# A two-layer graph attention kernel: the mean of a row without edges as one more product, and part of layer 1's weights on ScalarE

## The reference, cut to what matters

```python
h = relu(layernorm(x))                       # x: 8192 x 128
Whs, Wht, Whc = h @ Ws, h @ Wt, h @ Wc
e = Whs @ Wht.T                              # 8192 x 8192
alpha = softmax(where(adj > 0, e, -9e15))    # adj: int32, 0 or 1, about 8 ones in a row
x = x + alpha @ Whc                          # layer 0
h = relu(layernorm(x))
Wh = h @ W
e = leaky_relu((Wh @ a1)[:, None] + (Wh @ a2)[None, :], 0.2)
attention = softmax(where(adj > 0, e, -9e15))
x = x + elu(attention @ Wh)                  # layer 1
```

## Time and profile before

| | us |
|---|---|
| runs | 1568.74, 1573.38, 1574.76; median 1573.38 |
| profiled execution | 1571.87, span 1570.0 |
| PE busy | 1332.9 (85%) |
| DVE busy | 1372.5 (87%) |
| ACT busy | 854.9 (54%) |
| mean granted TensorE clock | 0.948 |

### The profile page before, as it was taken

One profiled execution on the slowest core, in us unless ns is written; L12 is line 12 of the kernel. 1 busy time (PEld: TensorE's weight loads), 2 busy tenths in 40 slices (PEclk: granted clock), 3 DMA queues, 4 the chain that ended last, 5 costly groups with the idle time before them and its releaser, 6 DMA issues. The chain is left out here.

```text
span 1570.0 us, 77864 instructions
## 1 busy us (share of the span) xinstructions
PE 1332.9 (85%) x31819; PEld 1156.7 (74%) x31819; DVE 1372.5 (87%) x2732; ACT 854.9 (54%) x1552; POOL 1.5 (0%) x11
## 2 busy tenths in 40 slices
PE   1736899999999999999999988686987887898885
PEld 1525778888888888888888877456887887887885
DVE  5776799999999999999999995357999899999997
ACT  1835566666676676676766665483432333333332
POOL 0000000000000000000000000000000000000000
PEclk9977899999999999999999999898998999999998
DMA  6058889999999999999999993102233232232331
GB/s 222 0 207 312 303 299 368 366 372 373 364 366 369 372 368 368 366 371 368 369 368 370 367 372 109 52 0 89 84 99 94 71 97 83 91 99 65 104 96 37
DMA packets 114303, 363.19 MB, mean 231 GB/s; under 512 B 11504, under 2 KB 44528, under 8 KB 81392
## 3 DMA queue, kind: packets, MB, share of 16 engines
q1 hardware_dynamic: 114160, 361.02, 64.5%
HBM read 319.03 MB, written 41.94 MB: 230 GB/s over the span
## 5 line engine op out<-in xcount | busy, mean ns | idle before, releaser
L799 PE MATMUL ps<-arena 128*128 128x129 f32 x2048 | 268.2, 293 | 31.7 <-DVE arena L1462 31.5
L1454 DVE TENSOR_SCALAR arena<-arena 128x128 f32 (+1 forms) x1024 | 267.9, 338 | 27.0 <-ACT arena L1040 26.7
L799 PEld LDWEIGHTS ps<-arena 128*128 128x128 f32 x2048 | 256.3, 207 | 41.2 <-DVE arena L1462 36.0
L722 PE MATMUL ps<-arena 128*128 128x129 f32 x2048 | 252.6, 282 | 2.8 <-DVE y_t L1361 1.7
L722 PEld LDWEIGHTS ps<-arena 128*128 128x128 f32 x2048 | 240.6, 196 | 10.4 <-issue 2.3
L1287 DVE TENSOR_SCALAR arena<-arena 128x2048 fp8e4<-128x2048 int32 x192 | 234.8, 1224 | 6.2 <-PE ps L679 2.5
L976 ACT ACTIVATE arena<-ps 128x512 f32<-128x512 f32 x256 | 153.4, 599 | 132.9 <-PE ps L664 132.8
L788 PE MATMUL ps<-arena 128*32 128x131 f16 x8192 | 157.9, 230 | 38.9 <-issue 28.2
L970 ACT ACTIVATE arena<-ps 128x512 f16<-128x512 f32 x256 | 153.6, 600 | 55.9 <-PE ps L652 55.8
L702 PEld LDWEIGHTS ps<-arena 128*128 128x128 f16 x2048 | 136.7, 98 | 63.4 <-issue 3.5
L1040 ACT ACTIVATE arena<-ps 128x393 f32<-128x393 f32 (+1 forms) x384 | 150.0, 462 | 54.9 <-PE ps L788 54.9
(11 more groups left out here) (147 smaller groups left out, 1378.0 us busy)
## 6 DMA issues: line engine op xcount, KB each, us to landing
arena<-in_adjB SPq DMA_DIRECT2D x256, 1024.0 KB, 7.5
sel_pick<-arena SPq DMA_DIRECT2D x64, 256.0 KB, 9.5
sel<-arena SPq DMA_DIRECT2D x64, 256.0 KB, 9.5
arena<-sel_pick SPq DMA_DIRECT2D x64, 256.0 KB, 3.1
arena<-sel SPq DMA_DIRECT2D x64, 256.0 KB, 2.7
x_t<-in_x SPq DMA_DIRECT2D x64, 64.0 KB, 7.4
x_mid<-y_t SPq DMA_DIRECT2D x64, 64.0 KB, 7.7
arena<-x_mid SPq DMA_DIRECT2D x8, 512.0 KB, 4.4
```

Source lines behind the costliest of these rows:

```text
L722: last = nc.tensor.matmul(pv_ps, p_T[:, s * P:(s + 1) * P], v_sel[:, b, s, :], start=(s == 0), stop=(s == SB - 1), skip_group_check=True)
L799: last = nc.tensor.matmul(xv_ps[b], w_msk[:, b, s, :], x1_sel[:, b, s, 0:VW], start=(s == 0), stop=(s == SB - 1))
L1454: last = nc.vector.tensor_scalar(w_raw[:, s, :], own, x1_sel[:, b, s, D + 2:D + 3], x1_sel[:, b, s, D + 1:D + 2], ALU.mult, ALU.max)
```

## The change

Three things are changed.

1. **The mean as first product.** The value of a row without edges no longer comes from a flag. The mean, times 2^-90, is split into three bfloat16 parts in three groups of partitions (`mean_parts`), with 2^-90 itself in the denominator's column. One bfloat16 matmul of ones with these rows starts each weighted sum, in both layers. Next to real weights 2^-90 is lost in rounding; without edges it is all there is, and the division gives the mean. So `denominator` is one reciprocal read from PSUM, the base `u_t` is gone from `finish`, and in layer 1 `finish_a` has neither the flag's product nor its addition. The bound that `decide` puts on small denominators goes from exp(-50) to exp(-30).
2. **Four of sixteen raw weights on ACT** (`bend`): slot groups 6 and 7 of each half. max(a*r, b) is written as relu(a*r - b) + b: a Relu with two per-partition operands and an Identity with one. For this each gathered row has one more column, -b (`XW` 132 instead of 131), and `w_raw` has two buffers. The masked product waits for `w_act` too.
3. **The finish of a batch in four pieces**: `finish_a` behind the first tile of the next batch, `above_zero` behind the third, `below_zero` behind the fourth, `finish_b` behind the fifth. SP loads x8 and stores a batch's result in the seventh tile instead of the fourth.

```diff
@@ PE: weigh; weigh_rows likewise with mean_rows[1]
+                    nc.tensor.matmul(pv_ps, ones_b[:, :], mean_rows[0], start=True, stop=False, skip_group_check=True)
...
-                                            start=(s == 0), stop=(s == SB - 1), skip_group_check=True)
+                                            start=False, stop=(s == SB - 1), skip_group_check=True)
@@ PE: selected_keys
+                pe.wait_ge(rows_ready, 2)
@@ SP: batch_io
-                    if u == 3:
+                    if u == 6:
@@ ACT
+            def bend(t, b, h):
+
+                act.wait_ge(xg_evac, t * 6 + (3 if h == 0 else 6))
+                wait(act, w_ready, t * 2 + (h - 3))
+                act.sem_inc(act_settled, 1)
+                own = r_row[:, bass.ts(t, P)]
+                for s in BENT:
+                    k = 8 * h + s
+                    last = nc.scalar.activation(w_raw[b][:, k, :], own, ACT.Relu, bias=x1_sel[:, b, k, D + 3:XW],
+                                                scale=x1_sel[:, b, k, D + 2:D + 3])
+                last.then_inc(bend_done, 1)
+                act.wait_ge(bend_done, t * 2 + (h + 1))
+                for s in BENT:
+                    k = 8 * h + s
+                    last = nc.scalar.activation(w_raw[b][:, k, :], w_raw[b][:, k, :], ACT.Identity,
+                                                bias=x1_sel[:, b, k, D + 1:D + 2])
+                last.then_inc(w_act, 1)
...
+                    for h in range(2):
+                        bend(t, u % 2, h)
@@ DVE: denominator and finish of layer 0
-                nc.vector.tensor_scalar(no_edge[:, 0, bass.ds(t, 1)], den, 0.0, None, ALU.is_equal
-                                        ).then_inc(flag_done, 1)
-                dve.wait_ge(flag_done, t + 1)
-                nc.vector.scalar_tensor_tensor(dens[:, bass.ds(t, 1)], den, TINY, no_edge[:, 0, bass.ds(t, 1)],
-                                               ALU.max, ALU.max).then_inc(den_done, 1)
-                dve.wait_ge(den_done, t + 1)
                 settle()
-                nc.vector.reciprocal(inv[:, 3:4], dens[:, bass.ds(t, 1)]).then_inc(inv_done, 1)
+                nc.vector.reciprocal(invs[:, bass.ds(t, 1)], pv_ps[:, D:VW]).then_inc(inv_done, 1)
...
-                nc.vector.scalar_tensor_tensor(u_t[:, 0, :], mean_v[:, 0, :], no_edge[:, 0, bass.ds(t, 1)],
-                                               x_t[:, b, :], ALU.mult, ALU.add).then_inc(base_done, 1)
@@ DVE: the mean's parts, made once before each layer
+            def mean_parts(rows, left, done):
+
+                done(nc.vector.tensor_copy(rows[:, 0:D], left[:, :]))
+                done(nc.vector.tensor_tensor(left[:, :], left[:, :], rows[:, 0:D], ALU.subtract))
+                nc.vector.tensor_copy(rows[32:64, 0:D], left[32:64, :])
+                done(nc.vector.tensor_copy(rows[64:P, 0:D], left[64:P, :]))
+                done(nc.vector.tensor_tensor(left[64:P, :], left[64:P, :], rows[64:P, 0:D], ALU.subtract))
+                done(nc.vector.tensor_copy(rows[64:P, 0:D], left[64:P, :]))
+                nc.vector.memset(rows[96:P, :], 0.0)
+                nc.vector.memset(rows[32:64, D:VW], 0.0)
+                nc.vector.memset(rows[64:96, D:VW], 0.0)
+                nc.vector.memset(rows[0:32, D:VW], UNIT).then_inc(rows_ready, 1)
@@ DVE: finish_a of layer 1
-                nc.vector.tensor_tensor(fin[:, 1, :], flag, tot[:, :, D], ALU.add).then_inc(fin1_done, 1)
-                nc.vector.tensor_tensor(y8[:, :, :], flag.unsqueeze(2).to_broadcast(full),
-                                        mean_v[:, 1, :].unsqueeze(1).to_broadcast(full), ALU.mult
-                                        ).then_inc(h8_part, 1)
...
-                nc.vector.tensor_tensor(y8[:, :, :], y8[:, :, :], tot[:, :, 0:D], ALU.add).then_inc(h8_part, 1)
@@ DVE: step of layer 1
-                    if u == 1 and (not isinstance(j, int) or j):
-                        finish_b(j - 1)
+                        if u == 2:
+                            above_zero(j - 1)
+                        if u == 3:
+                            below_zero(j - 1)
+                        if u == 4:
+                            finish_b(j - 1)
```

More of the change, by code:

```diff
@@ L28 @@
 SHIFT = 50.0
-TINY = 1e-30
+UNIT = 2.0 ** -90
+NONE = 2.0 ** 84
+DEPTH = 30.0
 EPS = 1e-5
@@ L38 @@
 QB = P // SLOT
-XW = D + 3
+XW = D + 4
+BENT = (6, 7)
 NO_EDGES = struct.unpack("<f", bytes([0xB0] * 4))[0]
@@ L95, in gnn_kernel @@
         mx_b = part(TOP + 2304, P)
+        mean_rows = [part(at, 65, BF16)[:, 0:VW] for at in (END, TOP + 2560)]
+        mean_left = part(END + 65, P)
         no_edge = part(TOP + 2432, 2 * TILES).rearrange("p (k t) -> p k t", k=2)
@@ L114, in gnn_kernel @@
         W1A = VS + 2 * SB * XW
-        w_raw = part(W1A, 2048).rearrange("p (s n) -> p s n", n=P)
+        w_raw = [part(at, 2048).rearrange("p (s n) -> p s n", n=P) for at in (W1A, 5120)]
         w_msk = part(W1A + 2048, 4096).rearrange("p (r s n) -> p r s n", r=2, n=P)
-        assert W1A + 6144 <= 6 * N
+        assert W1A + 6144 <= TOP + 2304 and 5120 + 2048 <= VALS
         m_in = part(MASK + 2048, 1024, F16).rearrange("p (r n) -> p r n", r=2)
@@ L279, in gnn_kernel @@
         w_made = sem("w_made")
+        bend_done = sem("bend_done")
+        act_settled = sem("act_settled")
+        w_act = sem("w_act")
         w_ready = sem("w_ready")
@@ L797, in weigh_rows @@
                     wait(pe, tot_in, t - 1)
+                    nc.tensor.matmul(xv_ps[b], ones_b[:, :], mean_rows[1], start=True, stop=False,
+                                     skip_group_check=True)
                 for s in range(8 * h, 8 * h + 8):
                     last = nc.tensor.matmul(xv_ps[b], w_msk[:, b, s, :], x1_sel[:, b, s, 0:VW],
-                                            start=(s == 0), stop=(s == SB - 1))
+                                            start=False, stop=(s == SB - 1), skip_group_check=True)
                 last.then_inc(xv_done, 1)
             def selected_keys():
+                pe.wait_ge(rows_ready, 2)
                 def step(j, u):
@@ L1381, in tile_step @@
                 if there(i, 4):
-                    denominator(d, b)
+                    denominator(d)
                 if there(i, 0):
@@ L1451, in weights @@
                     dve.wait_ge(xg_evac, t * 6 + (3 if h == 0 else 6))
-                    wait(dve, w_ready, t * 2 + (h - 1))
-                    for s in range(8 * h, 8 * h + 8):
-                        last = nc.vector.tensor_scalar(w_raw[:, s, :], own, x1_sel[:, b, s, D + 2:D + 3],
-                                                       x1_sel[:, b, s, D + 1:D + 2], ALU.mult, ALU.max)
+                    wait(dve, w_ready, t * 2 + (h - 3))
+                    for s in range(8):
+                        if s not in BENT:
+                            k = 8 * h + s
+                            last = nc.vector.tensor_scalar(w_raw[b][:, k, :], own, x1_sel[:, b, k, D + 2:D + 3],
+                                                           x1_sel[:, b, k, D + 1:D + 2], ALU.mult, ALU.max)
                     last.then_inc(w_made, 1)
@@ L1459, in weights, with chain_rows @@
                     dve.wait_ge(w_made, t * 2 + (h + 1))
+                    dve.wait_ge(w_act, t * 2 + (h + 1))
                     wait(dve, xv_done, t * 2 + (h - 3))
                     settle()
-                    nc.vector.scalar_tensor_tensor(w_msk[:, b, at, :], m_in8[:, b, at, :], 0.0, w_raw[:, at, :],
+                    nc.vector.scalar_tensor_tensor(w_msk[:, b, at, :], m_in8[:, b, at, :], 0.0, w_raw[b][:, at, :],
                                                    ALU.is_gt, ALU.mult).then_inc(w_ready, 1)
+            made = [0]
+            def chain_rows(ins):
+                made[0] += 1
+                ins.then_inc(parts_made, 1)
+                dve.wait_ge(parts_made, made[0])
             def compare():
@@ L1500, in finish_b, with below_zero @@
                                                ).then_inc(elu_part, 1)
+            def below_zero(j):
                 dve.wait_ge(h8_exp, j + 1)
                 nc.vector.tensor_scalar(e8[:, :, :], e8[:, :, :], 1.0, -1.0, ALU.min, ALU.add).then_inc(elu_part, 1)
+            def finish_b(j):
                 dve.wait_ge(elu_part, j * 2 + 2)
@@ L1506, in selected_keys @@
             def selected_keys():
+                mean_parts(mean_rows[1], mean_v[:, 1, :], chain_rows)
                 def step(j, u):
                     weights(j * STEPS + u, u % 2)
-                    if u == 0 and (not isinstance(j, int) or j):
-                        finish_a(j - 1)
-                    if u == 1 and (not isinstance(j, int) or j):
-                        finish_b(j - 1)
+                    if not isinstance(j, int) or j:
+                        if u == 0:
+                            finish_a(j - 1)
+                        if u == 2:
[4 more added lines that the diff above has]
+                            finish_b(j - 1)
```

59 lines of the change are left out of this document (30 added, 29 removed).

## The result

| | before | after |
|---|---|---|
| median of the runs compared | 1571.89 | 1518.41 (1515.84 to 1534.86) |
| ratio, 95% interval | | 0.968 (0.961 to 0.974) |
| profiled execution | 1571.87, span 1570.0 | 1534.86, span 1533.0 |
| PE, DVE, ACT busy | 1332.9, 1372.5, 854.9 | 1311.9, 1272.6, 1043.3 |

The forecast was 1519.

What follows compares the result with a forecast made beforehand. It took DVE to bound layer 1, PE close behind, and DMA to hold layer 0. Gains of 46.5 us (layer 1), 2.3 (last finish_a) and 4 (layer 0 and seams) off 1571.87 gave 1519 us; 8-in-10 range 1499 to 1542.

Steps and rivals of the forecast that it cites:

- Layer 1's pace: Layer 1: PE becomes the pace instead of DVE, with weighted sums 6.12 us apart.
- the eight activations: Layer 1, ACT: four Relus and four Identities per tile take 3.2 us (2.8 to 3.7), which barely fits.
- halfway between two rows: Layer 1, ACT: Identities 0.29 us apart, the middle between a copy without operands (0.18) and a Relu (0.41).
- The limits of 3.3 and 3.6 us: Layer 1, ACT: room for its activations until its next sum comes late (3.3), until its work exceeds PE's step (3.6).
- rival B: Layer 1: ACT sets the pace with a tile of 6.5 us, 24 us given back, 1543 us; chance 0.12.
- Jumps: Layer 1's loop: six jumps cost PE 5.4 us each beyond a tile, 32.4 in all, no longer hidden.
- the slower sum behind: Layer 1: the first sum after each jump runs at a lower clock, 0.4 us each, 2.6 for six.
- 3.4 of the jump: Layer 1 before the change: the part of a jump that reaches DVE, in its batch sum of 61.4 us.
- behind the layer's last sum: End of layer 1: the last finish_a is shorter by 2.3 us.
- The start and the mean's parts: Ahead of layer 0's sweep: small steps that make the mean's parts add 2.6 us, 0 if loads hide it.
- the missing hundredth: Layer 0: DMA share 0.99 leaves 0 to 8 us to gain, 5 taken; layer 0 and the seams together -4.
- Rival A: Layer 0: DMA share is not capacity and PE sets the pace, 24 us more off, 1495 us; chance 0.09.

Runs made afterwards that it cites:

- e11: The changed kernel with layer 1's batches written out and six of sixteen raw weights on ACT instead of four: 1533.81 us, ratio 0.977.
- e7: The changed kernel with layer 1's loop over batches written out on all engines, so no jump is taken in it: 1486.92 us, ratio 0.949.
- e10: The kernel before with the change in layer 1 only, and layer 1's batches written out: 1491.06 us, ratio 0.948.
- e5: The kernel before with layer 0's fourth adjacency chunk loaded for the first tile only and used again for all: 1559.92 us, ratio 0.995.
- e6: The changed kernel with layer 0's fourth adjacency chunk loaded for the first tile only and used again for all: 1477.60 us, ratio 0.941.
- e9: The kernel before with the change in layer 0 only, layer 1 as before: 1572.42 us, ratio 1.001.
- e2: The changed kernel with all sixteen raw weights on DVE and the finish undivided, leaving the mean as first product: 1552.42 us, ratio 0.987.
- e3: The changed kernel with all sixteen raw weights on DVE, the finish still in four pieces: 1550.56 us, ratio 0.984.
- e4: The changed kernel with the finish undivided, four raw weights still on ACT: 1532.92 us, ratio 0.974.
- e8: The changed kernel measured once more, unaltered, on another occasion: 1516.85 us, ratio 0.966 to the kernel before.

## Why the prediction was right

**Layer 1's pace.** Predicted 6.12 us between sums, measured 6.05: 64 times 0.07 is 4.5 us to the good. The mean's product and the wider selection cost 0.03 together, where 0.10 was taken; the product alone puts 0.06 in front of the sum. PE is the pace, DVE waits for ACT, the waits for masked weights are gone: each as forecast.

**ACT.** 3.1 us for the eight activations against 3.2. A pair of Relus takes 0.87, of Identities 0.69; with the rows of e11 (three Relus 1.26, three Identities 0.99) a further Relu adds 0.39 and an Identity 0.30 (0.41 and 0.29 taken). The Identity had been placed halfway between two rows, and it was there. By the Trainium skill, "ScalarE: Activation LUTs", section "What ACT_TABLE_LOAD costs", a per-partition operand is worth about 93 ns: the difference between the two, 0.09, agrees. The limits of 3.3 and 3.6 us were sound: at 3.1 ACT is back 0.28 us before the sum is there (its wait at 1165.79), and e11 puts the second limit at 6.05 - 2.32 = 3.7. What rival B was feared for, "only 0.1 us lies between my 3.2 and the 3.3", was the first, and passing that one alone would delay a copy and not yet PE. That is argued from these limits; no run has five weights on ScalarE.

**Jumps.** 5.4 us each, taken whole: the sums on either side of a jump are 5.7 us further apart than a tile in the mean of the first profile and 5.8 in the second; written out, they give back 5.2 (e7) or 4.7 (e10) each. The forecast had read 5.7 before the change and took 0.4 of it for the slower sum behind. That was a slip: the 11.71 us end where the slower sum starts, so the 0.4 come on top, and 5.7 was the term. Its check of DVE's batch (61.4) also used a remainder, "3.4 of the jump"; in the timeline that it reads DVE waits 3.93 us there, and that batch takes 63.2 us from jump to jump. By the Trainium skill, "Runtime: NRT & Kernel Launch", section "Instruction fetch mechanics", the stall belongs to the taken jump. The runs agree: writing the batches out takes 31 and 28 us off.

**The term that was missing.** Layer 1 came to 444.8 and 440.6 against 439.3, although its tile was 4.5 us cheaper over the layer. What offsets it are the jumps, about 2 us over what was taken for the six, and gaps inside batches, in straight code (1222.15 is one), which the sum had at nothing. In the first profile PE stands seven times in straight code, 5.7 us in all; in the second twice, 1.0 us. So a batch is 56.8 and 56.1 us in the mean where 55.5 was forecast. The profile of the kernel before had such gaps already, three between 1080 and 1500 us, 2.6 us in all, which cost little there because DVE set the pace.

**finish_a.** 1.52 against 1.7; behind the layer's last sum 2.5 less against 2.3.

**The start and the mean's parts.** Predicted +2.6, with 0 if the loads hide it: measured +3.0 at the first indicator (98.79 to 101.75), 2.5 of it the parts themselves and the rest a step before them that came later in that execution. The sweep behind is no shorter for it (852.5 and 852.0 in the mean), so the loads do not hide it.

**Layer 0.** This is the mis-sized term. The forecast had DMA hold the tile, and e5 and e6 show that it does; but it still put 5 us down for "the missing hundredth" of the DMA share, 4 net. Measured: net +1, 3 either way (e9), and a sweep that is 0.5 us shorter in the mean of the profiles. Where the share is 0.99, the missing hundredth was not capacity that a quicker DVE could use. By the Trainium skill, "DMA: Bandwidth & Descriptors", section "Where 436 GB/s comes from", HBM gives a core about 358 GB/s. By that rule layer 0 gains nothing, and the outcome is nearer to that than to the sum, though the traces move 361 to 372. Rival A's mechanism (PE at 12.5) needed less data, which only e6 had.

**The ledger.** 53.5 us between the medians, 52.8 forecast. The experiments share it out, one part after another: the mean's product 19.5 (1571.9 to e2's 1552.4), the spread finish 1.9 (to e3's 1550.6), ScalarE's weights 32.2 (to 1518.4). These are medians from different chips, each is uncertain by several us, and the shares hold for this order alone: in the other one, e2 to e4 and then to the changed kernel, ScalarE's weights get 19.5 and the spreading 14.5. Layer 1's sums, first to last, are steadier: 28 to 31 us for the weights in either order, 1.5 to 5 for the spreading. Place by place, between the profile before and the second one of the changed kernel (48.8 us apart by their spans, 1570.0 and 1521.2): layer 1 45.2, behind its last sum 2.5, layer 0's sweep 3.3, its start -3.0, the passage between the layers 0.6 (118.1 to 117.5), in all 48.6. The closeness of 52.8 is partly luck: the forecast gave layer 1 from 1 to 5 us too much and layer 0 some 4 too much, and that execution, like the first profiled one, is longer than its kernel's median (by 7 us). What makes up the 7 us between it and the median no profile shows.

**Not settled.** Whether layer 0 gained two or three us after all: the means of the sweeps say no, but in e9's profile it is 3.4 us shorter than before (100.26 to 950.46), while layer 1, whose work is that of before, is 8.9 us longer (494.7). Why runs of one kernel differ: the changed one from 1515.84 to 1534.86 and again from 1514.08 to 1525.78, the one before from 1565.55 to 1578.81 over the 17 runs beside e8. Layer 0's sweep is 7.5 us longer in the changed kernel's slowest profile than in the second one, at the same work, and layer 1 4.2. Nor was it tried what sets the gaps inside straight code; in e7 the row selection has three of them left, 4.5 us in all, one of 3.1. And no run writes the batches out in the kernel before, so what the jumps cost there, with DVE as the pace, is open.

## What to carry to other kernels

Where one engine is the pace by a third of a microsecond and the next stands behind it, price the second first: the gain of relieving the first is the distance to the second, here 6.37 to 6.05, plus what the first did beside its loop. A loop with two bounds at one place (DVE 13.1, DMA 13.2) gains nothing from the removal of one; reducing the other's load in both kernels, as e5 and e6 do, shows it in one pair of runs. And once PE is the pace, look at the jumps of its loop: writing the batches out (1486.92) gave more than half of what the whole change did.

## What the runs showed that was not expected

- PE stands for 0.2 to 1.2 us in straight code inside a loop's body with nothing to wait for. In the loop of the changed kernel that is at two places only, behind the 7th product of a sum and behind the 60th of a row selection, in some batches and not in others; in e4 it is the first of them in each of the loop's seven batches. It did so before the change too:

```profile
1162.52 0.30 PE L788 MATMUL ps<-arena 128*32 128x131 f16 x8 [0.69 <-issue]
```

- This loop became irregular when DMA came to hold it, though its mean is steady. Most tiles of layer 0 before were 13.10 or 13.16 us; in the changed kernel they alternate around 12.5 and 13.9, some at 15.5, with a mean of 13.17 and 13.18. With a quarter less to load and PE as the pace (e6) most are even again, 12.46 to 12.50.
- The same layer 1 varies from execution to execution by more than its tile does: 444.8 and 440.6 us in the changed kernel, 485.8 before and 494.7 in e9, which has the layer 1 of before.
